# A new order of work within a row and in the prologue of an AdaLN retention and expert-FFN kernel

## The reference, cut to what matters

```python
def reference(...):
    h = _layernorm(x) * (1 + ca) + sa
    # attention part: decayed running mean over time, a 256x256 product, and a 5-tap conv
    a = sigmoid(decay_logit)
    S_t = a * S_{t-1} + (1 - a) * h_t
    x = x + ga * (S @ W.T + b + conv5(h, conv_w) + conv_b)
    # feed-forward part: one of 8 experts for each row, chosen from the last token
    h = _layernorm(x) * (1 + cb) + sb
    sel = argmax(softmax(gelu(h[:, -1] @ Wp1 + bp1) @ Wp2 + bp2))
    g = gelu(h @ W1[sel] + b1[sel])
    out = (g @ W2[sel] + b2[sel]) @ Wo + bo
    return x + gb * (h + 0.3 * out)
```

## Time and profile before

| | |
|---|---|
| median of 3 runs | 676.41 us (676.09 to 677.36) |
| profiled execution | 675.09 us, of which its span 673.0 us |
| PE busy | 656.8 us (98%) |
| DVE busy | 566.8 us (84%) |
| ACT busy | 568.2 us (84%) |
| POOL busy | 464.5 us (69%) |
| PE clock granted | 0.989 of full on the mean |

### The profile page before, as it was taken

The page is one execution under the profiler, slowest core; times in us unless marked ns, Lnnn a source line. Parts: engine busy times, 40 slices in busy tenths (PEclk is TensorE's granted clock), DMA queues, the critical chain, the costliest instruction groups (busy, mean ns, idle before and its releaser), DMA issues.

```text
span 673.0 us, 11162 instructions
## 1 busy us (share of the span) xinstructions
PE 656.8 (98%) x3469; PEld 525.2 (78%) x3469; DVE 566.8 (84%) x863; ACT 568.2 (84%) x976; POOL 464.5 (69%) x536
## 2 busy tenths in 40 slices
PE   8989999999999999999999999999999999999996
PEld 7877777777878777777788777777787877777764
DVE  1698799999999999999999999999999999998611
ACT  3788788888998888888898888888899888887753
POOL 2885477787767777778776777778777777777543
PEclk7899999999999999999999999999999999999999
DMA  8998455565454555556544565555544554544551
GB/s 291 362 369 271 157 160 186 157 188 184 133 163 156 180 178 167 167 179 188 155 145 158 171 188 160 182 160 189 175 142 156 162 179 174 173 132 150 164 167 46
DMA packets 55454, 120.58 MB, mean 179 GB/s; under 512 B 5643, under 2 KB 43364, under 8 KB 46180
## 3 DMA queue, kind: packets, MB, share of 16 engines
q1 hardware_dynamic: 51844, 115.65, 53.9%
q10 hardware_dynamic: 3552, 4.23, 2.0%
HBM read 61.12 MB, written 25.19 MB: 128 GB/s over the span
## 4 chain that ended last, share of the span: by engine, by line
PE 89%; ACT 3%; DVE 2%; DMA 2%; issue 1%; POOL 1%; ACTq 0%; POOLq 0%; SPq 0%; DVEq 0%
PE Q L1073 10%; PE Q L1068 9%; PE U L1053 9%; PE U L1055 9%; PE U L1054 9%; PE Q L1069 8%; PE TR L1093 8%; PE Y L1037 5%; PE TR L1085 4%; PE Q L1085 4%; PE Y L1033 4%; PE Y L1034 4%; PE Q L1018 3%; PE U L1108 2%; DMA xn<-in_L_attn_W_dram 1%
## 5 line engine op out<-in xcount | busy, mean ns | idle before, releaser
L454 POOL TENSOR_TENSOR g_lo<-g,g_hi 128x512 fp32r<-128x512 f32 x128 | 190.8, 1500 | 140.8 <-ACT g_hi L614 135.1
L836 DVE SCALAR_TENSOR_TENSOR Y<-h,taps,Y 128x512 f32<-128x512 f32 x320 | 222.5, 750 | 2.9 <-PE Y L1037 0.6
L1068 PE MATMUL Q<-g_hi,down_w 128*128 128x512 f32 x256 | 109.8, 429 | 0.2
L1053 PE MATMUL U<-hid_hi,up_w 128*128 128x512 f32 x256 | 106.1, 414 | 0.0
L607 ACT ACTIVATE g<-U,up_w 128x512 f32<-128x512 f32 x128 | 88.6, 692 | 18.7 <-PE U L1055 15.8
L1069 PE MATMUL Q<-g_hi,down_w 128*128 128x512 f32 x256 | 101.2, 395 | 0.0
L1055 PE MATMUL U<-hid_lo,up_w 128*128 128x512 f32 x256 | 100.8, 394 | 0.0
L1054 PE MATMUL U<-hid_hi,up_w 128*128 128x512 f32 x256 | 100.7, 393 | 0.0
L881 DVE TENSOR_TENSOR_SCAN S<-keep,h 128x512 f32<-128x512 f32 x64 | 76.3, 1231 | 28.0 <-ACT h L684 28.0
L566 ACT ACTIVATE S<-xr,nmr,rstd 128x256 f32<-128x256 f32 x128 | 66.7, 592 | 38.5 <-POOL S_lo L462 36.3
L784 DVE BATCH_NORM_STATS2 st<-xr 128x6 f32<-128x512 f32 x128 | 87.7, 706 | 11.4 <-DMA xr<-in_L_attn_x_dram 7.0
(11 more groups left out here) (116 smaller groups left out, 1290.1 us busy)
## 6 DMA issues: line engine op xcount, KB each, us to landing
up_w<-up_table SPq DMA_DIRECT2D x32, 1027.0 KB, 6.7
down_w<-down_tab SPq DMA_DIRECT2D x32, 1024.0 KB, 8.7
xr<-in_L_attn_x_dram SPq DMA_DIRECT2D x32, 512.0 KB, 3.5
out_dram<-xr SPq DMA_DIRECT2D x64, 256.0 KB, 2.3
xr<-in_L_ffn_W_dram ACTq DMA_DIRECT2D x5, 512.0 KB, 8.3
xr<-in_L_ffn_W_dram SPq DMA_DIRECT2D x4, 512.0 KB, 7.4
up_table<-g_lo SPq DMA_DIRECT2D x2, 1024.0 KB, 9.4
up_table<-down_w SPq DMA_DIRECT2D x2, 1024.0 KB, 10.5
```

The source lines that it names most:

```text
L454: nc.gpsimd.tensor_tensor(g_lo[:, f], g[:, f % 2], g_hi[:, f].bitcast(f32), ALU.subtract).then_inc(g_lo_ready, 1)
L836: ins = nc.vector.scalar_tensor_tensor(out=Y[c][:, :], in0=h[:, c, k:k + T], scalar=taps[:, c, k:k + 1], in1=Y[c][:, :], op0=ALU.mult, op1 ...
L1053: mm(U[f % 2][:, :], up_w[:, par, UP + w:UP + w + P], hid_hi[:, par, c], start=(c == 0), stop=False)
L1068: mm(Q[c][:, :], down_w[:, par, 1, w:w + P], g_hi[:, f], start=(f == 0), stop=False)
```

## The change

Only the order of steps changes; no step is added, removed or resized.

In the loop:
- PE: `out_to_tokens` moves from behind mix to behind up 0 and up 1, directly ahead of the xn2 transposes; the first half of up 2 moves ahead of down 0.
- ACT: gelu 0 and gelu 1 come ahead of both casts of g; `gate1` moves behind `h_of`; the two casts of S stand together behind the last cast of g.
- DVE: the first tap of conv moves ahead of `output`, four taps follow it, and `stats1` moves between the fifth and the sixth tap; `s_low1` moves behind the second half of `residual1`.
- POOL: `gate_beta` moves from ahead of `hid_low` to behind `norm1`.

In the prologue the steps are put in another order on every queue. On SP, four loads of weights go ahead of the small vectors and of the first row, and the transfers out of the split W1 are spread otherwise. PE takes the first modulation ahead of the vectors' transpose and W's transposes ahead of those of W2. The router of row 0 and the third combine stand at other places.

The core of the diff:

```diff
@@ SP, prologue
+                load_w1(0)
+                load_w()
+                load_w1(1)
+                load_w2(0)
                 vectors()
                 load_x(0)
-                load_w2(0)
-                load_taps()
 
                 for_modulations()
-                load_w1(0)
...
@@ POOL, slot
                     g_low(i, 0)
                     g_low(i, 1)
-                    gate_beta(i)
                 if row(i + 1):
                     hid_low(i + 1)
                 if row(i + 4):
                     norm1(i + 4)
                 if row(i):
+                    gate_beta(i)
                     g_low(i, 2)
                     g_low(i, 3)
@@ ACT, slot
                     gelu(i, 0)
+                    gelu(i, 1)
                     g_high(i, 0)
-                    gelu(i, 1)
                     g_high(i, 1)
...
-                if row(i + 2):
-                    gate1(i + 2)
                 if row(i):
                     gelu(i, 2)
                 if row(i + 3):
                     h_of(i + 3)
+                if row(i + 2):
+                    gate1(i + 2)
                 if row(i):
                     g_high(i, 2)
-                if row(i + 3):
-                    s_high(i + 3, 0)
-                if row(i):
                     gelu(i, 3)
                     g_high(i, 3)
                 if row(i + 3):
+                    s_high(i + 3, 0)
                     s_high(i + 3, 1)
@@ DVE, slot
+                if row(i + 2):
+                    conv(i + 2, 0, 1)
                 if row(i - 1):
                     output(i - 1)
                 if row(i + 2):
-                    conv(i + 2, 0, CONV_HEAD)
+                    conv(i + 2, 1, 5)
                 if row(i - 1):
                     residual2(i - 1)
-                if row(i + 2):
-                    conv(i + 2, CONV_HEAD, TAPS * DC)
                 if row(i + 4):
                     stats1(i + 4)
+                if row(i + 2):
+                    conv(i + 2, 5, TAPS * DC)
...
                     residual1(i + 2, 0)
+                    residual1(i + 2, 1)
                 if row(i + 3):
-
                     s_low1(i + 3)
-                if row(i + 2):
-                    residual1(i + 2, 1)
@@ PE, prologue
+                modulation(0)
                 vec_transpose()
-                modulation(0)
                 modulation(1)
                 modulation(2).then_inc(s_mod_mm, 1)
+                w_transposes()
@@ PE, slot
                     mix(i + 2)
-                if row(i - 1):
-                    out_to_tokens(i - 1)
                 if row(i):
                     up(i, 0)
                     up(i, 1)
+                if row(i - 1):
+                    out_to_tokens(i - 1)
                 if row(i + 1):
                     to_channels(i + 1, xn, xn2_ready, t3_done)
                 if row(i):
+                    up(i, 2, (0,))
                     down(i, 0)
-                    up(i, 2, (0,))
```

More of the change, by code:

```diff
@@ L507, in prologue @@
                 w1_lo(1)
+                s_low0(0)
+                gates()
                 norm1(1)
-                s_low0(0)
                 w1_lo(2)
                 w1_lo(3)
-                gates()
                 w1_lo(4)
-                norm1(2)
                 s_low0(1)
@@ L518, in prologue @@
                 w1_lo(6)
+                norm1(2)
                 w1_lo(7)
@@ L694, in prologue @@
                 down_high(0, 0)
+                s_high(0, 0)
+                w1_hi(2)
+                down_high(0, 1)
                 w2T_copy(1)
-                s_high(0, 0)
-                down_high(0, 1)
-                w1_hi(2)
+                s_high(0, 1)
                 w1_hi(3)
-                s_high(0, 1)
                 down_high(1, 0)
+                w1_hi(4)
                 w2T_copy(2)
                 xn1_of(1)
+                w2T_copy(3)
                 down_high(1, 1)
-                w1_hi(4)
-                w1_hi(5)
-                down_high(2, 0)
-                down_high(2, 1)
-                w2T_copy(3)
-                h_of(1)
-                gate1(0)
+                down_high(2, 0)
+                gate1(0)
+                h_of(1)
+                down_high(2, 1)
+                s_high(1, 0)
+                w1_hi(5)
+                w2T_copy(4)
+                s_high(1, 1)
                 down_high(3, 0)
-                s_high(1, 0)
-                s_high(1, 1)
-                w2T_copy(4)
+                down_high(3, 1)
                 w1_hi(6)
                 w2T_copy(5)
-                down_high(3, 1)
                 down_high(4, 0)
-                xn1_of(2)
-                w1_hi(7)
-                xn2_of(0)
-                down_high(4, 1)
-                hid_of(0)
-                w2T_copy(6)
-                down_high(5, 0)
-                hid_high(0)
-                h_of(2)
-                gate1(1)
-                w2T_copy(7)
-                s_high(2, 0)
-                down_high(5, 1)
+                xn2_of(0)
+                w1_hi(7)
+                down_high(4, 1)
+                w2T_copy(6)
+                hid_of(0)
+                xn1_of(2)
+                down_high(5, 0)
+                gate1(1)
+                down_high(5, 1)
+                w2T_copy(7)
+                down_high(6, 0)
+                h_of(2)
+                nav_of(0)
+                s_high(2, 0)
+                hid_high(0)
                 s_high(2, 1)
-                down_high(6, 0)
-                nav_of(0)
                 down_high(6, 1)
@@ L887, in prologue @@
                 mods_setup()
-                stats1(1)
+                mix_low()
                 scan(0, 0)
-                betas()
+                scan(0, 1)
                 down_low(0, 0)
                 down_low(0, 1)
-                scan(0, 1)
-                mix_low()
+                betas()
                 s_low1(0)
+                stats1(1)
                 down_low(1, 0)
                 dve.wait_ge(s_taps, 16)
-                conv(0, 0, 6)
+                conv(0, 0, 10)
                 down_low(1, 1)
-                conv(0, 6, 9)
                 down_low(2, 0)
-                conv(0, 9, 10)
-                stats1(2)
+                scan(1, 0)
                 down_low(2, 1)
-                scan(1, 0)
                 scan(1, 1)
@@ L908, in prologue @@
                 down_low(3, 0)
-                s_low1(1)
                 residual1(0, 1)
                 down_low(3, 1)
+                s_low1(1)
+                stats1(2)
                 down_low(4, 0)
@@ L915, in prologue @@
                 conv(1, 6, 10)
+                down_low(5, 0)
+                down_low(5, 1)
                 scan(2, 0)
-                down_low(5, 0)
                 scan(2, 1)
+                down_low(6, 0)
+                router(0)
                 residual1(1, 0)
-                down_low(5, 1)
-                down_low(6, 0)
+                down_low(6, 1)
                 stats1(3)
-                router(0)
-                down_low(6, 1)
+                s_low1(2)
+                down_low(7, 0)
                 residual1(1, 1)
-                down_low(7, 0)
                 down_low(7, 1)
-                s_low1(2)
             def slot(i):
+                if row(i + 2):
+                    conv(i + 2, 0, 1)
                 if row(i - 1):
@@ L1146, in prologue @@
                 w2_transposes(4)
+                comb(2, 1)
                 comb(3, 0)
```

52 lines of the change are left out of this document (24 added, 28 removed).

## The result

| | before | after |
|---|---|---|
| median | 676.25 us (675.50 to 677.36) | 701.72 us (700.49 to 702.97) |
| profiled execution | 675.09 us, span 673.0 | 702.97 us, span 701.0 |

The ratio is 1.0383, 95% interval 1.0365 to 1.0400: slower by 25.5 us. The forecast was 693.5 us with a range of 662 to 699. The direction and the mechanism in the loop came as forecast; the prologue did not, and the time lies 2.7 us outside the range.

The account below looks back on a forecast made before the run. TensorE was taken as the bound, only its waits to be won or lost. Profiled 675.1 + 21.0 (28 slots) - 0.8 (slots 28, 29) - 3.0 (end) + 0 (prologue) = 692.3; plus 1.3: 693.5 us, range 662 to 699.

Parts of the forecast that it names:

- part 1: Loop slot: first scan falls between norm1's two small steps, shuts out second step and pow; g_lo late, +0.75 us per slot.
- Rival A: Loop: second small step gets in before the scan, only the pow is shut out; -0.32 us per slot, 664 us, chance 0.30.
- The size per slot: Loop: PE's wait for g_lo grows to 1.01 us from 0.25, +0.75 per slot, +21.0 us over 28 slots.
- the tail from the pow's true start to g_lo: POOL in a slot: 1.33 us from pow's start to next g_lo, plus some 0.22 for the moved gate_beta.
- The page of the skill: Scan against POOL: whole-instruction exclusion would make the slot 0.2 us longer, the sum 5.6 us higher; prediction used 1.01 us.
- parts 2 and 3: Last slots: 28 and 29, without norm1, lose both waits, -0.8 us; 30 and 31 lose waits for rT, -3.0 us.
- two ups stand ahead of them: Slots 30 and 31: two ups (2.8 us) ahead of the output transposes cover the 1.8 us waits for rT.
- part 4: Prologue: later vectors against earlier norm, scans and router 0; taken as 0, with 3 us either way.
- the prediction's own sign for it: Start of loop: a first slot starting more than 3 us from 71 us would make the prologue's forecast wrong.
- up to 5.1 us more before vec_transpose: Prologue: 1.75 MB of large loads ahead of the small vectors, at 346 GB/s; partly covered by modulation 0.
- Rival C: Scan comes before norm1's first step, both small steps caught, g_lo 2 another 0.2 us late, bad prologue: 702 us, chance 0.08.

Follow-up runs that it names:

- psum_three: slots_only with three more VectorE maxima, read from PSUM and used by nobody, ahead of the router's own: 664.49 us, ratio 0.9831.
- psum_two: slots_only with two more VectorE maxima, read from PSUM and used by nobody, ahead of the router's own: 687.31 us, ratio 1.0179.
- scan_later: slots_only with three tiny unused VectorE operations (two columns each, SBUF on both sides) ahead of the first scan: 703.28 us, ratio 1.0392.
- vectors_first: prologue_only with the seven small vectors issued ahead of the four large loads: 678.76 us, ratio 1.0049.
- prologue_only: The changed kernel's prologue with the loop of the kernel before: 684.83 us, ratio 1.0121.
- after_mended: The full change, with the first scan waiting for both small steps of norm1 (exchanged) and the small vectors issued first: 671.88 us, ratio 0.9947.
- gate_back: slots_only with gate_beta back in its old place on POOL, ahead of hid_low: 692.46 us, ratio 1.0245.
- small_six: scan_later with six small VectorE operations, SBUF on both sides, instead of three ahead of the scan: 705.80 us, ratio 1.0436.
- slots_only: The changed kernel's loop with the prologue of the kernel before: 692.37 us, ratio 1.0229.

## Why the prediction was right in the loop and wrong in sum

**The meeting (part 1): right, step by step.** With t counted from the first matmul of mix (335.77), forecast and measured stand so. The forecast's times leave out w, the wait of mix for S_lo (0.17), which it took to shift everything alike; the measured ones hold it (0.18: the pair takes 0.65 for 0.47). So the second column is to be compared with the third.

| | forecast, without w | forecast with w | measured |
|---|---|---|---|
| first small step of norm1 | 12.25 | 12.42 | 12.34 |
| first scan | 12.42 | 12.59 | 12.58 |
| second small step | 12.55 | 12.72 | 12.66 |
| next g_lo starts | 16.12 | 16.29 | 16.11 |
| PE's low-part matmul of down 2 | 17.45 | 17.62 | 17.45 |

The scan fell between the two steps, as forecast; it is 0.08 us ahead of the second in this slot and 0.07 to 0.14 in all, for 0.13. Rival A (664 us) needed the scan 0.15 later or POOL earlier by as much; psum_three moved the scan, and gave 664.5 us. The pow rows at 2.00, the small step at 0.23 and slots of 18.42 (forecast 18.5) are those that A named. A's total is met in part by luck: its gain in the loop is there (-9.7 us over slots 0 to 27, forecast -9.6), its 3 us at the end are not (below). So A was a fair rival: the change lost a race that some 0.2 us decide (from about 0.1 behind to the 0.09 ahead that psum_two shows to be enough).

**The size per slot: 0.75 forecast, 0.60 measured.** From PE's low-part matmul of down 2 to the next mix are 1.97 us (353.22 to 355.19), before 1.96, so a slot is longer by as much as that matmul is later. With w it was forecast at 17.62 and came at 17.45; that it meets the 17.45 without w is chance. The mis-sized term is the tail from the pow's true start to g_lo: 1.55 us forecast (1.33, and 0.22 for gate_beta), 1.42 measured (350.46 to 351.88). Another 0.05 come from the second scan, which starts 1.12 us after the first for 1.14, keeps POOL out for 0.99 for 1.01, and from the first, earlier by 0.01. Over slots 0 to 27 this makes 16.5 us in place of 21.0.

**The page of the skill.** The Trainium skill, SBUF — State Buffer, section "Who interferes with whom", has a DVE instruction with two SBUF inputs and a GpSimd instruction that reads SBUF exclude each other for the whole instruction. In the trace of after, the pow caught by the second scan (which starts at 349.47 and takes 1.19) ran from 350.46, its end at 351.50 less its usual 1.04: 0.99 us after the scan's start, not the scan's whole 1.19. By the whole instruction the slot would have been about 0.2 us longer (an estimate, the difference of the two). On who is excluded trace and page agree; on how long, the trace decides, as the prediction took it. But scan_later shows that a step can also miss the short opening between two scans: one with 0.23 us of work, there since 342.54, ran only in the last 0.23 us before 344.99.

**The end (parts 2 and 3): -0.8 and -3.0 forecast, -0.5 and 0.0 measured.** Slots 28 and 29 are shorter by 0.34 and 0.12 us. From the last matmuls of slot 29 to the end are 38.3 us in both kernels (634.69 to 673.0, 662.71 to 701.0). The wait for rT did shrink as forecast (one of 1.8 us left). In its place came another, in the last two slots (start, us, operation, and the wait in brackets, then the chain):

```profile
664.83 0.50 PE L1048 MATMUL U<-hid_hi,up_w 128*128 128x512 f32 x1 [1.49 <-DMA up_w<-up_table]
```

```profile
657.98 6.81 DMA up_w<-up_table
```

The last slots have no mix, and out_to_tokens no longer stands at their head, so PE reaches up 0 sooner than the expert's table is there: the router's choice, then a transfer of 6.8 us. Two such waits, this and one at 681, make 3.0 us and cancel the gain. The step that failed here is "two ups stand ahead of them": it asked what PE would do while rT is made, and not whether the ups' own operands are there.

**The prologue (part 4): 0, with 3 either way, forecast; +12.0 measured.** This is the step that put the time outside the range, and the prediction's own sign for it came: a first slot more than 3 us from 71. The prediction saw the place, the small vectors behind 1.75 MB of weights, and priced it at up to 5.1 us more before vec_transpose (7.1 measured). It stopped there, and then let other moves cancel it. What the traces show are three links. That the first brings on the second is read from the rows, and that mending the first removes the last is shown by vectors_first; that the second leads to the third is in part argued:

1. The vectors. PE, against 6.23 and a wait of 0.28 before:

```profile
13.32 0.35 PE L977 MATMUL U<-ident,vec_rows 57*128 57x57 f32 x1 [2.76 <-DMA vec_rows<-in_L_ffn_bp_dram]
```

The vectors are 7.1 us later. Modulation 0 stands ahead and covers part of it, 2.76 us are a wait of PE. The modulations end at about 20.5 instead of 14.3.

2. SP's queue. SP waits for the modulations before it issues the next loads, 3.2 us before, now 8.9:

```profile
SPq L286 <- PE Y L985: 8.9, 1, 8.9
```

The DMA engines, which before were fully busy here, run dry. The table of stretches from 18 to 22 us (length, busy us by engine, clock, DMA share, GB/s), before and then after:

```profile
18.00:22.00 4.00, 4.00 (x18) 3.88 (x18) 1.38 (x3) 2.65 (x5) 2.61 (x2) 0.50 1.09 361
```

```profile
18.00:22.00 4.00, 4.00 (x21) 4.00 (x21) 0.88 (x6) 3.04 (x6) 3.24 (x2) 1.00 0.08 17
...
62.00:70.00 8.00, 6.32 (x24) 5.75 (x25) 0.05 (x1) 4.31 (x8) 0.00 (x0) 0.57 1.10 348
```

361 GB/s became 17. (361 - 17) x 4 us = 1.4 MB not moved, some 3.8 us of the full rate, in a stretch whose transfers are wanted until the end of the prologue. At 30 us 8.2 MB have been moved, before 9.5.

3. A late W2. The W2 of the last expert but one is issued at 45.86 us, by ScalarE's queue, and lands 17.8 us later (a row of the chain). It meets SP's late transfers only in the transfer engines:

```profile
45.86 17.77 DMA xr<-in_L_ffn_W_dram
```

```profile
63.69 1.97 PE L962 MATMUL U<-ident,xr 128*128 128x128 f32 x8 [6.12 <-DMA xr<-in_L_ffn_W_dram]
```

PE waits 6.1 us, and in the stretch that follows the granted clock from 62 to 70 us is 0.57 of full on the mean: part of these matmuls run at the lower of the two levels (eight transposes take 1.97 us here, 1.04 in the loop), after an engine that had just been idle. From this matmul to the next transposes of a W2 are 8.19 us (63.69 to 71.88); the same instructions took 5.20 in vectors_first (57.97 to 63.17), so the lower clock costs some 3 us on top of the wait. In prologue_only the wait was 2.5 us and the clock from 62 to 70 us 0.86; this is where the full change and its half differ. Their gap from 18 to 22 us is alike, with 8.2 MB moved at 30 us in both. Then, from 30 to 50 us, the transfer engines are busy all the time in both, but move 283 GB/s in the full change and 325 in prologue_only (377 before). So the gap alone does not make the 6.1 us, and why the rate was lower stays open. The four runs of the full change lie 2.5 us apart, so how far the delay grows is not the same each time.

vectors_first shows that the order of the vectors starts it: with that mended, the SP wait falls from 8.1 to 0.6 us, the W2 is there in time, and about 5.5 of 7.9 us return. In after_mended, beside the new slots, the first mix starts at 74.19 us: the one moved call gives back 8.9 of the 12.0 us. It also shows which link costs. Up to the matmuls ahead of that W2 PE is no earlier with the vectors first (it starts them at 56.25 us, in prologue_only at 55.56 and in the full change at 55.68), so its own wait for the vectors is not what was lost; all of the gain comes behind that point. The prediction's error was not the 5.1 us but to end a delay where it is first seen. It should have asked what SP has queued behind the wait for PE, and then what the prologue still wants from the transfer engines late. With -4.5 us in the loop, +0.3 in slots 28 and 29, +3.0 at the end and +12.0 here, the span grew by 10.8 us more than forecast; the step between median and profiled execution, taken as +1.3 and now -1.25, hid 2.6 of them.

**Rival C (702 us) has the measured time, 701.7, for other reasons.** It took the first small step to be caught and a prologue worse by 3 us. Here the second was caught, the loop came out better than forecast, and the prologue was worse by 12. C's loop price for a first step caught, another 0.2 us per slot, is borne out by gate_back (0.19 us more from the scan to the end of the pow, and 19.43 us or more against the 19.25 of slot 1); it did not come about in the full change.

## What to carry to other kernels

When a reordering brings the steps of two engines within a few tenths of a microsecond of each other, look whether they exclude each other in SBUF; if they do, fix their order with a wait or a small shift, since a race lost by 0.1 us can be lost in every slot (here 1.7% of the time to be won, or 2.3% lost). When a load is delayed, follow the delay through the issuing queue: what that queue waits for, what stands behind it, and whether the transfer engines run dry meanwhile. And before work is moved ahead of a wait, check that the moved work's own operands are there.

## What the runs showed of the hardware

- The lead that a GpSimd step of 0.23 us needs over a scan is known here to about 0.01 us: with 0.02 to 0.08 it is caught, with 0.08 to 0.11 it passes (psum_two, 27 slots; one slot passes with 0.08). In gate_back leads of 0.02 to 0.08 are caught in 26 of 27 slots, in psum_three 0.10 to 0.19 pass in all. In the kernel before, the pow passes with 0.10 to 0.18.
- Small VectorE operations with SBUF on both sides ahead of the scan raise that lead: leads of 0.05 to 0.12 are caught in all 27 slots of scan_later, 0.25 to 0.27 in six slots of small_six. How they do it was not settled.
- A GpSimd step with 0.23 us of work took 2.45 us beside two back-to-back scans (scan_later), where in slots_only one that came 0.09 us after the first scan got in between the two (1.14 us). That a waiting step can miss the opening was not expected. All cases of it stood beside those small operations; whether they are the reason was not tested by itself.
- The other way round it depends on the operation. The scan of the earlier trace rows at 329.79, 0.11 us into a pow of 1.04, is not held: the two scans take 2.34 us, in the trace of after 2.31. In the prologue of the kernel before a scan starts at 21.91, inside a GpSimd operation on 128x1024 elements (20.48, 2.35 us), and takes 2.00 us instead of about 1.2.
- The modulation matmuls of 128x32 show a rate that the clock row does not explain. Before, and after (two matmuls each):

```profile
8.21 0.39 PE L990 MATMUL Y<-silu_cT,g 128*128 128x32 f32 x2
```

```profile
8.24 0.61 PE L985 MATMUL Y<-silu_cT,xr 128*128 128x32 f32 x2
```

Before, pairs follow each other every 0.22 us at a granted clock of 1.00, and from 9 us on every 0.43 at 0.51. After, they follow every 0.43 us from 6.97 on, and eight transposes at 23.04 still take 1.91 us (1.04 in the loop), but the record says 1.00 all that time. Here the record of the clock and the spacing of the matmuls don't fit each other; the spacing is that of the lower level. It was not followed up. Of the pairs that ran at the faster spacing before, eight are modulation 0 (1.8 us then, 3.4 now, covered by the wait for the vectors) and four are modulation 1, which cost 0.8 us more.
